# Two mamba-and-FFN decode stages on one Trainium2 core: ScalarE and VectorE get instruction orders of their own for the stages that decode weights

## The reference

```python
    x = x + _layernorm(_L0_attn_ref(_layernorm(x), W_in, conv_w, conv_b, W_out, A_log, D_param, dt_bias))
    x = x + _layernorm(_L0_ffn_ref(_layernorm(x), lut, gate_idx, up_idx, down_idx))
# the scan inside _L0_attn_ref, per token:
    S = S * dA_t[:, :, None, None] + jnp.einsum('bh,bn,bhp->bhpn', dt_t, B_t, x_t)
    y_t = jnp.einsum('bhpn,bn->bhp', S, C_t)
# inside _L0_ffn_ref: each weight is lut[idx]; INTER = 1376
    gate = _ghost_linear(x, gate_idx, lut)
    up = _ghost_linear(x, up_idx, lut)
    h = jax.nn.silu(gate) * up
    return _ghost_linear(h, down_idx, lut)
```

## Time and profile before

| | us |
|---|---|
| median of 3 runs | 1444.87 |
| lowest and highest | 1444.31, 1446.34 |
| the profiled execution | 1443.4 |
| its span in the trace | 1441.7 |
| start, up to stage 0 | 61.2 |
| stages 0 and 1 (decode stages) | 310.2 |
| from stage 2 to the end | 1070.3 |

### The profile page before, as it was taken

How to read it: one execution, slowest core, us unless ns; L and a number is a source line. 1 busy time by engine, 2 the same in 40 slices (tenths; PEclk the granted TensorE clock), 3 DMA queues, 4 the chain that set the end, 5 groups by cost and what they waited for, 6 DMA issues and landing times. The chain is left out here.

```text
span 1441.7 us, 19103 instructions
## 1 busy us (share of the span) xinstructions
PE 1361.3 (94%) x6912; PEld 672.6 (47%) x6912; DVE 933.8 (65%) x1869; ACT 577.1 (40%) x1018; POOL 457.6 (32%) x691
## 2 busy tenths in 40 slices
PE   4878987988999999999999999999999999999998
PEld 2334444444554445444545445544554444444443
DVE  7978866987577656765676567755775555544432
ACT  5466655676444234332434243423442233122120
POOL 1312233333233434334322433254334242310102
PEclk9889998999999999999999999999999999999999
DMA  5133233322310223013301320032102110311201
GB/s 164 37 102 88 69 93 100 92 75 56 74 45 23 59 70 85 19 36 93 73 16 52 88 71 26 23 92 77 44 23 71 39 44 23 97 43 30 74 1 51
DMA packets 99021, 87.79 MB, mean 61 GB/s; under 512 B 68208, under 2 KB 68208, under 8 KB 98928
## 3 DMA queue, kind: packets, MB, share of 16 engines
q1 hardware_dynamic: 97040, 86.54, 21.8%
q10 hardware_dynamic: 1888, 0.03, 0.1%
HBM read 54.05 MB, written 16.78 MB: 49 GB/s over the span
## 5 line engine op out<-in xcount | busy, mean ns | idle before, releaser
L1312 PE MATMUL bank<-fxt,ffn_hi 128*128 128x512 f16 (+1 forms) x1408 | 418.8, 379 | 2.0 <-DVE dn L1677 1.5
L1312 PE MATMUL bank<-fxt,ffn_lo 128*128 128x512 f16 (+1 forms) x704 | 266.8, 379 | 0.0
L1312 PEld LDWEIGHTS bank<-fxt,ffn_hi 128*128 128x128 f16 (+1 forms) x1408 | 139.8, 100 | 173.1 <-issue 12.9
L1210 PE MATMUL bank<-mask,diag 128*128 128x416 f16 x640 | 128.0, 354 | 21.7 <-ACT ffn_lo L830 20.2
L605 POOL TENSOR_TENSOR state<-state,ex 64x512 f32<-64x512 f32 x32 | 36.8, 1149 | 343.3 <-PE bank L1265 342.3
L1326 PE MATMUL bank<-ffn_hi,h_hi 128*128 128x512 f16 (+1 forms) x352 | 133.5, 379 | 0.0
L1326 PE MATMUL bank<-ffn_hi,h_lo 128*128 128x512 f16 (+1 forms) x352 | 133.4, 379 | 0.0
L1326 PE MATMUL bank<-ffn_lo,h_hi 128*128 128x512 f16 (+1 forms) x352 | 133.3, 379 | 0.0
L1643 DVE SCALAR_TENSOR_TENSOR gact<-gact,bank 128x512 f32<-128x512 f32 (+1 forms) x88 | 60.2, 684 | 105.7 <-ACT gact L874 104.8
L874 ACT ACTIVATE gact<-bank,c_gate_half 128x512 f32<-128x512 f32 (+1 forms) x88 | 59.9, 681 | 154.7 <-PE bank L1312 153.1
L1496 DVE TENSOR_SCALAR mask<-codes_h 128x832 f16<-128x832 f16 x320 | 111.7, 408 | 12.5 <-PE bank L1210 12.2
(11 more groups left out here) (184 smaller groups left out, 2357.3 us busy)
## 6 DMA issues: line engine op xcount, KB each, us to landing
codes_sb<-codes SPq DMA_DIRECT2D x80, 208.0 KB, 3.4
ures<-u SPq DMA_DIRECT2D x32, 256.0 KB, 2.8
x_scratch<-x SPq DMA_DIRECT2D x32, 256.0 KB, 2.0
ut<-x_scratch SPq DMA_DIRECT2D x16, 512.0 KB, 4.3
xres<-x_scratch SPq DMA_DIRECT2D x32, 256.0 KB, 3.0
out<-dn SPq DMA_DIRECT2D x32, 256.0 KB, 2.1
ut<-u SPq DMA_DIRECT2D x15, 512.0 KB, 4.4
ffn_hi<-w_in_t SPq DMA_DIRECT2D x4, 580.0 KB, 9.2
```

The costliest lines, as they stand in the source:

```text
L1210: last = nc.tensor.matmul(p.bank[:, 0:COLS], diag[:, q].rearrange("p n m -> p (n m)"), mask[:, n, q, j * COLS:(j + 1) * COLS], start=(q == ...
L1312: last = nc.tensor.matmul(bank, wt[:, c0:c0 + w], fxt[:, :, half, k, :], start=(k == 0 and n == 0), stop=(k == KC - 1 and n == 2))
```

## The change

`stage(t)` of ACT and of DVE is split: `decode_stage(t)` serves stages 0 and 1 and `stage(t)` the rest. The programs of PE, POOL and SP stay as they are, instruction for instruction. In the stages from 2 on ACT and DVE have the order that they had; only line numbers move (L1496 becomes L1506 and so on). In the decode stages no instruction is added or taken away, and each keeps its waits; they stand in another order:

- ACT: each cast of codes stands one decoded piece later or more. `codes_to_half(k + 4)`, which was first in the stage, stands behind `decoded(t, 0)`, the others follow, with the last, k + 23, ahead of `decoded(t, 19)`. The copy of transposed y and of the projected y stand ahead of casts. `conv_tanh` of blocks 0, 2 and 3 stand later, behind copies of decoded pieces, and `normalise_slice("x", ...)` stands behind `decoded(t, 13)` in Q2 and behind `out_projected(t, 3)` in Q3.
- DVE: in Q0 `masks(k + 3)` moves ahead of `out_weights_low` (stage 0 only) and of `ln_split`; in Q1 `weigh` moves ahead of `conv(t + 1, 4)`, `decayed` ahead of `masks`, and `time_steps` behind `masks(k + 9)` and `conv(t + 1, 0)`; in Q2 and Q3 `decayed` moves ahead of masks and masks move between each `conv` and its `conv_silu`; in Q3 `ln_split("x", ...)` stands behind `masks(k + 20)`.

```diff
@@ ACT, decode_stage(t)
+                def decode_stage(t):
+                    ffn_next = t >= 1
+                    k = half_unit_count(t, 0)
+
+                    decoded(t, 0)
+                    codes_to_half(k + 4)
+                    small(t, 1)
+                    decays(t, 1)
+                    if t >= 1:
+                        normalise(t - 1, 3)
+                    normalise_slice("u", t + 1, 0, 0)
+                    normalise_slice("u", t + 1, 0, 1)
+                    decoded(t, 1)
+                    y_transposed(t, 0)
+                    codes_to_half(k + 5)
+                    decoded(t, 2)
+                    out_projected(t, 0)
+                    codes_to_half(k + 6)
+                    normalise_slice("u", t + 1, 1, 0)
+                    normalise_slice("u", t + 1, 1, 1)
+                    decoded(t, 3)
+
+                    decoded(t, 5)
+                    codes_to_half(k + 8)
+                    dt_input(t + 1)
+                    conv_input(t + 1, 4)
+                    normalise(t, 0)
+                    dt_exponential(t + 1)
+                    small(t, 2)
+                    decays(t, 2)
+                    conv_tanh(t + 1, 4)
+                    codes_to_half(k + 9)
+                    decoded(t, 6)
+                    y_transposed(t, 1)
+                    codes_to_half(k + 10)
+                    conv_input(t + 1, 0)
+                    decoded(t, 7)
+                    out_projected(t, 1)
+                    decoded(t, 8)
+                    codes_to_half(k + 11)
+                    conv_tanh(t + 1, 0)
+                    codes_to_half(k + 12)
+                    decoded(t, 9)
+
+                    decoded(t, 10)
+                    conv_input(t + 1, 1)
+                    normalise(t, 1)
+                    small(t, 3)
+                    decays(t, 3)
+                    conv_tanh(t + 1, 1)
+                    codes_to_half(k + 14)
+                    decoded(t, 11)
+                    conv_input(t + 1, 2)
+                    y_transposed(t, 2)
+                    conv_input(t + 1, 3)
+                    codes_to_half(k + 15)
+                    decoded(t, 12)
+                    conv_tanh(t + 1, 2)
+                    out_projected(t, 2)
+                    decoded(t, 13)
+                    codes_to_half(k + 16)
+                    conv_tanh(t + 1, 3)
+                    codes_to_half(k + 17)
+                    if ffn_next:
+                        normalise_slice("x", t - 1, 0, 0)
+                        normalise_slice("x", t - 1, 0, 1)
+                    decoded(t, 14)
+
+                    decoded(t, 15)
+                    codes_to_half(k + 18)
...
@@ DVE, decode_stage(t) against the decode lines of the old stage(t)
                     weigh(t, 1)
                     decayed(t, 1)
+                    masks(k + 3)
                     if t == 0:
                         out_weights_low()
                     ln_split("u", t + 1, 0, 0)
                     ln_split("u", t + 1, 0, 1)
-                        masks(k + 3)
                     masks(k + 4)
                     ln_stats("u", t + 1, 1)
                     masks(k + 5)
...
                     y_split(t, 1, k + 7)
                     dt_input(t + 1)
-                        conv(t + 1, 4)
                     weigh(t, 2)
-                        masks(k + 8)
+                    conv(t + 1, 4)
                     decayed(t, 2)
+                    masks(k + 8)
                     conv_silu(t + 1, 4)
-                        time_steps(t + 1)
                     if ffn_next:
                         ln_stats("x", t - 1, 0)
                     masks(k + 9)
                     conv(t + 1, 0)
-                        conv_silu(t + 1, 0)
+                    time_steps(t + 1)
                     masks(k + 10)
+                    conv_silu(t + 1, 0)
                     masks(k + 11)
@@ DVE, decode_stage(t)
+                    conv(t + 1, 1)
+                    weigh(t, 3)
+                    decayed(t, 3)
+                    masks(k + 13)
+                    conv_silu(t + 1, 1)
+                    conv(t + 1, 2)
+                    masks(k + 14)
+                    conv_silu(t + 1, 2)
+                    conv(t + 1, 3)
+                    masks(k + 15)
+                    conv_silu(t + 1, 3)
...
+                    y_split(t, 3, k + 17)
+                    weigh(t + 1, 0)
+                    decayed(t + 1, 0)
+                    masks(k + 18)
```

More of the change, by code:

```diff
@@ L906, in stage @@
[L906 to L912 removed]
+                    high(g, 1)
+                    normalise(t - 1, 3)
+                    gate_tanh(g, 2)
                     y_transposed(t, 0)
[L914 removed]
+                    if nxt:
@@ L927, in stage @@
[L927 to L939 removed]
+                    high(g, 2)
+                    gate_tanh(g, 3)
@@ L1127, in _ @@
                 codes_to_half(3)
-                for t in range(TILES):
+                for t in range(LAG):
+                    decode_stage(t)
+                for t in range(LAG, TILES):
                     stage(t)
@@ L1692, in stage @@
                     y_gated(t, 0)
-                    if ffn:
-                        times_up(g, 0)
-                    y_split(t, 0, k + 2 if dec else None)
-                    if ffn and nxt:
+                    y_split(t, 0, k + 2)
+                    weigh(t, 1)
+                    decayed(t, 1)
+                    masks(k + 3)
+                    if t == 0:
+                        out_weights_low()
+                    ln_split("u", t + 1, 0, 0)
+                    ln_split("u", t + 1, 0, 1)
@@ new lines, in decode_stage @@
+                    masks(k + 4)
+                    ln_stats("u", t + 1, 1)
+                    masks(k + 5)
+                    ln_split("u", t + 1, 1, 0)
+                    ln_split("u", t + 1, 1, 1)
+                    masks(k + 6)
+                    y_sum(t, 1)
+                    out_stats(t, 0)
+                    y_gated(t, 1)
+                    y_split(t, 1, k + 7)
+                    dt_input(t + 1)
+                    weigh(t, 2)
+                    conv(t + 1, 4)
+                    decayed(t, 2)
@@ new lines, in decode_stage, with stage @@
+                    masks(k + 19)
+                    z_gate(t + 1, 1)
+                    masks(k + 20)
+                    if ffn_next:
+                        ln_split("x", t - 1, 1, 0)
+                        ln_split("x", t - 1, 1, 1)
+                    ln_stats("u", t + 2, 0)
+                    z_gate(t + 1, 2)
+                    z_gate(t + 1, 3)
+                    masks(k + 21)
+                def stage(t):
+                    g = t - LAG
+                    nxt = t + 1 < TILES
+                    y_sum(t, 0)
+                    out_stats(t - 1, 3)
+                    gate_silu(g, 0)
+                    y_gated(t, 0)
+                    times_up(g, 0)
+                    y_split(t, 0)
+                    if nxt:
```

352 lines of the change are left out of this document (123 added, 229 removed).

## The result

The changed kernel takes 1477.26 us (median of 4 runs, 1475.67 to 1478.18) where the kernel before takes 1445.16 (4 runs). The ratio is 1.0228, with a 95% interval from 1.0203 to 1.0253. The forecast was 1442.8 and its range ended at 1449.0, so the prediction was wrong in sign and in size.

A forecast was written before the change was run, and what follows sets the result against it. PE bounds the kernel from 540 us on, so only stages 0 and 1 could gain, with DVE pacing Q1. Terms +1.2 + 2.5 - 3.3 - 2.7 + 0.3, unrounded -2.1, took 1444.87 to 1442.8 us; range 1435.5 to 1449.0.

The forecast's parts named there:

- Q1: Second quarter of stages 0 and 1: DVE paces and PE runs ahead; -2.0 and -1.3 us, together -3.3.
- On DVE: weigh now comes first: In Q1 weigh waits for gram until 269.4, where DVE before began the taps at 268.03: +1.4 us.
- the three signs given as "wrong": Stage 1's Q0 transposing DMA leaving before 238; DVE's idle time in Q1 and Q2 not shrinking; Q0's clock share rising.
- Q0: First quarter of both stages: the gain is taken back; stage 0 +2.5 us, stage 1 +1.2.
- The pair's path: In Q0, normalising the next tile's second pair holds piece 3's copy; stage 1's piece 4b starts only 0.2 us earlier.
- the term for half rate: In Q0, PE restarts at half rate at piece 4b after one merged wait: +1.4 us in each stage.
- half rate spreads: Rival: restarts cost 2.6 us at both pieces 4b, two further restarts 2.3 each; sum +4.9, 1449.8 us, chance 0.19.
- Q2: Third quarter: ACT reads block 2 sooner and the wait before piece 14b goes; stage 0 -1.1 us, stage 1 -1.6.
- Q3: Last quarter waits for z; in stage 0 POOL's products fall on y's split: +0.3 us.

The follow-up runs named there:

- the first mended kernel: The changed kernel with only ACT's cast of code piece k + 8 moved back ahead of decoded(t, 5): 1453.03 us, ratio 1.0065.
- the first three moves of ACT: Kernel before, ACT only: decoded(8) and projected y ahead of cast k + 12 and tanh; block 2's read ahead of cast k + 16; decoded(13) ahead of x's normalising: 1440.56 us.
- the two places mended: The changed kernel with the cast of k + 8 ahead of decoded(5) and decoded(3) ahead of the second pair's normalising: 1445.59 us, ratio 1.001.

## Why the prediction was wrong, by its own steps

**Q1, the step that failed.** "On DVE: weigh now comes first" and the sum that follows assume that PE runs ahead in Q1 and DVE sets the pace. The rule that refutes it stood in the description of the kernel before: SP's `load_codes(k)` waits for the cast of k - 2, and what stands behind it in SP's queue waits too. I followed that rule for `load_codes(k + 7)` and the first transposing DMA, and for nothing else. The second transposing DMA stands behind `load_codes(k + 10)`, and thus behind the cast of k + 8, which the change moves across `decoded(t, 4)` and `decoded(t, 5)`. The prediction names the cast of k + 8 nowhere. Its cost could be worked out from durations of the same kind: the last two copies and the cast 2.1, the load 1.1, the DMA's issue and landing 4.8, together 8 us from the end of piece 5, in both stages. Instead of the -3.3 us forecast for the two quarters Q1 the trace has +19.3, and moving the cast back by one piece takes 20.8 off them. Two of the three signs given as "wrong" are in the trace: DVE's idle time in Q1 grows from 3.7 and 3.4 us to 19.8 and 19.4, and the clock share in Q0 rises a little (0.77 to 0.80, 0.86 to 0.89).

**Q0, the wait right, the half rate mis-sized.** The pair's path came nearly as worked out: the first transposing DMA of stage 1 goes out 20.3 us behind the scan (20.1 forecast, 18.8 before), and one wait of 10.69 stands for the short ones. That DMA then keeps SP's queue for 3.10 us where it kept it for 1.83, so the second pair's load goes out later than forecast, which is most of the 1.7 us by which Q0 of stage 1 missed. But the term for half rate was 1.4 us, taken from the row where only eight matmuls followed the wait at half rate. Here 1.2 GHz lasts over piece 4b, the whole scan and part of piece 5. The kernel before has the same groups at full rate behind its wait of 0.26 us:

```profile
255.44 1.12 PE L1265 MATMUL bank<-state,cs 64*128 64x512 f32 x2
256.49 2.00 PE L1269 MATMUL bank<-xdt,decay 128*128 128x64 f32 x16
258.42 1.07 PE L1275 MATMUL bank<-xtok,gram 128*64 128x512 f32 x2
259.42 2.99 PE L1210 MATMUL bank<-mask,diag 128*128 128x416 f16 x16
```

Against 2.07, 3.67, 1.97 and 3.44 after, that is 0.95 + 1.67 + 0.90 + 0.45 = 4.0, and with 1.4 for piece 4b 5.4 us, of which 4.0 fall into Q1. They do not only lengthen PE: DVE adds the state behind the scan, and in the first mended kernel it does so 7.6 us behind the scan's start where it was 4.1. This is the rival "half rate spreads", which had 2.6 us for such a restart and a chance of 0.19. Even that was too little, and its time of 1449.8 did not have the queue. The Trainium skill (TensorE: Matmul & The Clock Gate, The HAM clock gate) has the full rate come back only after sustained work. The rows agree in kind. But one row could not give the price, and the length of the wait does not give it either. In stage 0 of the kernel before, a wait of 2.78 us was followed by half rate (1.03 us for the two matmuls of block 3) where stage 1 had the full rate after 2.77, and the last section has restarts behind waits of 3.56 to 8.73 us that cost between 1.4 and 5.9 us, both ends behind nearly the same program and the same wait of 3.56.

**Q2, the stretch right, its start wrong.** From the start of block 1's tanh to PE's block 3 I had 4.5 us for 6.25, and it is 4.63 (348.30 - 343.67). But the tanh comes late. ACT's timeline has it waiting for DVE, and the normalising ahead of it for POOL, which needs DVE's statistics:

```profile
337.17 0.81 ACT L868 ACTIVATE x<-x,obias,oscale 128x512 f32<-128x512 f32 x1 [3.57 <-POOL obias L619]
...
343.67 0.63 ACT L792 ACTIVATE cin<-xs 128x512 f32<-128x512 f32 x1 [3.94 <-DVE xs L1534]
...
347.56 0.69 ACT L778 ACTIVATE cin<-bank,c_in 128x512 f32<-128x512 f32 x1
```

DVE begins y_sum(2) 9.8 us behind the scan (330.39 - 320.57); before it was 1.9 us (295.43 - 293.52). I had let DVE gain in Q1 and start Q2 no later than before, and it starts 7.9 us later. A part of this is only moved: without the stall before piece 9b PE reaches the scan of Q2 earlier and DVE does not. The kernel with the first three moves of ACT, which takes that stall away and leaves the queue and DVE alone, has Q1 5.1 us shorter and Q2 4.3 and 4.1 longer. PE waits the difference off before block 3, and the matmuls behind that wait run at half rate (1.03 us for the two that took 0.60 in the earlier trace rows), as forecast.

**What held.** The stall before piece 9b is gone. ACT's waits for masks at casts fall from 49.7 us to 5.8. Q3 and the time from stage 2 on are as forecast. The 44 us of waiting that the change took off ACT bought nothing: with the two places mended the kernel takes what it took before (ratio 1.001). The view of waits has the 5.8:

```profile
ACT codes_h L819 <- DVE mask L1506: 5.8, 2, 5.4
```

**What stays open.** Why DVE's new order costs 17 us beside ACT's old one is read from rows for Q0 of stage 1 (4.3 us) and open for the rest. Why it costs nothing beside ACT's new order and helps beside the mended one is open too, and so is how much of Q2's growth is the moved stall. The 24 and 7.4 us account for the 32 in this sequence of mends; since the orders act on each other, other sequences would divide it otherwise.

## What to carry to other kernels

When an instruction is moved, list every wait on its semaphore, every queue in which such a wait stands, and for each queue all that stands behind the wait, down to the next consumer on the engine that bounds the kernel. Do it for each moved instruction and not for the first alone. Here one cast of 1 us, moved back past one piece, was worth 24 us. Two engines' orders are one design: a new order on one has to be measured with the other's new order, and a sum of the two alone tells little (+32 and +17 us alone, +32 together). A wait taken away on the bounding engine may come back one quarter later, so look at the whole stretch and not at the quarter.

## What the runs showed of the hardware

The cost of a restart of TensorE is not one figure, and the length of the wait does not set it. Behind waits of 10.69, 10.46 and 6.30 us the eight matmuls of a half piece took 2.95 to 2.96 us instead of 1.58, and the scan after them was at half rate as well (2.07 and 3.67 us for 1.12 and 2.00). In the run with the copy of piece 3 ahead this is what remained in stage 1:

```profile
252.31 2.96 PE L1220 MATMUL bank<-mask,diag 128*128 128x416 f16 x8 [6.30 <-ACT ffn_lo L830]
255.19 2.07 PE L1275 MATMUL bank<-state,cs 64*128 64x512 f32 x2
257.19 3.67 PE L1279 MATMUL bank<-xdt,decay 128*128 128x64 f32 x16
```

In the scan's first two groups alone that is 2.6 us (0.95 + 1.67) on top of the wait.

Behind the wait of 3.56 us before piece 9b the kernel before had 2.94 us for the eight matmuls and then the full rate in stage 1, 1.4 us in all, and in stage 0 2.56 us and 1.79 for the scan's first group, 1.7 in all. The run with the casts of k + 8 and k + 9 late has the same wait before the same piece in stage 1, behind the same groups of matmuls, and stays at half rate through the whole scan and into the next piece:

```profile
309.32 2.95 PE L1210 MATMUL bank<-mask,diag 128*128 128x416 f16 x8 [3.56 <-ACT ffn_lo L830]
312.21 2.07 PE L1265 MATMUL bank<-state,cs 64*128 64x512 f32 x2
314.21 3.67 PE L1269 MATMUL bank<-xdt,decay 128*128 128x64 f32 x16
317.81 1.97 PE L1275 MATMUL bank<-xtok,gram 128*64 128x512 f32 x2
319.71 4.01 PE L1210 MATMUL bank<-mask,diag 128*128 128x416 f16 x16
```

Against the full rate (1.58, 1.12, 2.00, 1.07 and 2.99) that is 5.9 us. And a long wait can be cheap: in the run with SP's DMA ahead of the load, a wait of 8.73 us in stage 0 cost 1.5 us. Its Q1 lasts 32.3 us there, against 36.8 in the run with the cast moved, where the scan was at half rate. That its execution is the fastest of its ten (1447.8 us) fits, but no run isolates the effect.

```profile
102.52 2.96 PE L1221 MATMUL bank<-mask,diag 128*128 128x416 f16 x8 [8.73 <-ACT ffn_lo L831]
105.41 1.27 PE L1276 MATMUL bank<-state,cs 64*128 64x512 f32 x2
```

So a forecast that merges waits should carry a range for each restart, here 1.4 to 5.9 us, and not one figure. What decides within the range, the runs don't tell.
